# Layer 1's queries: projected already turned, for two tiles at once, in half steps, in three of its four groups

## The reference

```python
x = x + tanh(g_xattn[0]) * xattn0(layernorm(x), ctx, ...)     # 32 heads of 128, 8 kv heads, q and k normalized
x = x + tanh(g_ffn[0])   * lora(layernorm(x), ...)            # 8 experts of rank 16
x = x + tanh(g_xattn[1]) * xattn1(layernorm(x), ctx, ...)     # 16 heads of 96, 4 kv heads
x = x + tanh(g_ffn[1])   * ffn(layernorm(x), ...)             # silu(x Wg) * (x Wu), 1792 wide, then Wd
# xattn1: hidden = concat(context, latents)                   # 128 + 128 rows per batch
q = (latents @ Wq.T).reshape(b, q_len, H, HD)                 # H = 16, HD = 96
k = (hidden @ Wk.T).reshape(b, s_len, KV, HD)                 # KV = 4
v = (hidden @ Wv.T).reshape(b, s_len, KV, HD)
attn = softmax(einsum('bkgqd,bksd->bkgqs', q, k) / sqrt(HD))
out = einsum('bkgqs,bksd->bkgqd', attn, v) @ Wo.T
```

## Time and profile before

| | us |
|---|---|
| median of 3 runs | 1289.67 |
| lowest, highest | 1287.07, 1289.84 |
| the profiled execution | 1286.68 |
| its span, first to last instruction | 1284.9 |
| PE busy | 1254.5 (98%) |
| DVE busy | 962.4 (75%) |
| ACT busy | 830.0 (65%) |
| POOL busy | 583.7 (45%) |

### The profile page before, as it was taken

One profiled execution on the slowest core, in us unless ns is written; L12 is line 12 of the kernel. 1 busy time (PEld: TensorE's weight loads), 2 busy tenths in 40 slices (PEclk: granted clock), 3 DMA queues, 4 the chain that ended last, 5 costly groups with the idle time before them and its releaser, 6 DMA issues.

```text
span 1284.9 us, 24439 instructions
## 1 busy us (share of the span) xinstructions
PE 1254.5 (98%) x7392; PEld 1101.7 (86%) x7392; DVE 962.4 (75%) x2425; ACT 830.0 (65%) x2867; POOL 583.7 (45%) x1029
## 2 busy tenths in 40 slices
PE   8899999999999999999999989999999999999998
PEld 7788888888888888888888878889999999878886
DVE  7887777787777777777777888887777778963433
ACT  5777777777777777677777654566676666732221
POOL 4566556565565566555566542422333323540000
PEclk9899999999999999999999999999999999999999
DMA  6675566454554554654555332243543324370000
GB/s 181 127 128 119 90 128 117 99 119 103 124 105 103 118 115 87 134 112 84 122 114 116 83 70 42 67 77 60 103 92 74 78 60 104 72 176 1 33 1 33
DMA packets 339078, 121.11 MB, mean 94 GB/s; under 512 B 307104, under 2 KB 325280, under 8 KB 338976
## 3 DMA queue, kind: packets, MB, share of 16 engines
q1 hardware_dynamic: 313888, 84.59, 34.6%
q10 hardware_dynamic: 21104, 29.12, 7.9%
q0 software_dynamic: 3984, 6.29, 2.1%
HBM read 39.21 MB, written 2.10 MB: 32 GB/s over the span
## 4 chain that ended last, share of the span: by engine, by line
PE 52%; DVE 18%; ACT 13%; POOL 6%; DMA 6%; issue 5%; ACTq 0%; SPq 0%; DVEq 0%; POOLq 0%
PE bank L576 13%; PE bank L578 13%; PE bank L577 13%; PE bank L817 7%; DVE split L1220 6%; DMA turned<-scratch 4%; PE bank L835 4%; DVE scratch L1294 3%; ACT scratch L942 3%; POOL rq L1676 3%; ACT scratch L917 3%; ACT bank L905 3%; DVE mx L1303 3%; ACT pieces L954 2%; ACT split L871 1%
## 5 line engine op out<-in xcount | busy, mean ns | idle before, releaser
L576 PE MATMUL bank<-split 128*128 128x256 f32 (+6 forms) x2120 | 703.9, 332 | 14.5 <-DVE split L1220 8.4
L577 PE MATMUL bank<-split 128*128 128x256 f32 (+6 forms) x2120 | 692.4, 327 | 0.0
L578 PE MATMUL bank<-split 128*128 128x256 f32 (+6 forms) x2120 | 692.1, 326 | 0.0
L576 PEld LDWEIGHTS bank<-split 128*128 128x128 f32 (+2 forms) x2120 | 402.2, 190 | 63.7 <-DVE split L1220 18.6
L578 PEld LDWEIGHTS bank<-split 128*128 128x128 f32 (+2 forms) x2120 | 402.0, 190 | 35.1
L577 PEld LDWEIGHTS bank<-split 128*128 128x128 f32 (+2 forms) x2120 | 402.5, 190 | 31.0
L1657 POOL CAST split<-turned 128x512 fp32r<-128x512 f16 x384 | 234.3, 641 | 289.6 <-DMA turned<-pieces 287.8
L871 ACT ACTIVATE split<-bank 96x256 fp32r<-96x256 f32 (+6 forms) x392 | 165.1, 432 | 80.9 <-PE bank L671 44.8
L1220 DVE TENSOR_TENSOR split<-bank,split 96x256 fp32r<-96x256 f32 (+6 forms) x392 | 185.0, 474 | 26.1 <-ACT split L871 19.4
L942 ACT ACTIVATE scratch<-bank,nb,w_max 128x256 f32<-128x256 f32 x256 | 141.5, 564 | 73.3 <-DVE nb L1306 73.2
L1326 DVE SCALAR_TENSOR_TENSOR pieces<-scratch,rs,pieces 128x256 f16<-128x256 f32 x384 | 175.0, 509 | 4.5 <-ACT pieces L954 2.2
(11 more groups left out here) (82 smaller groups left out, 1205.7 us busy)
## 6 DMA issues: line engine op xcount, KB each, us to landing
raw<-in_wq_a ACTq DMA_DIRECT2D x14, 512.0 KB, 4.3
raw<-in_wo_a ACTq DMA_DIRECT2D x14, 512.0 KB, 3.8
raw<-in_wkv_a ACTq DMA_DIRECT2D x7, 512.0 KB, 6.7
turned<-pieces SPq DMA_TRANSPOSE x192, 3.3
raw<-in_wq_c ACTq DMA_DIRECT2D x8, 384.0 KB, 3.3
craw<-in_ctx_t SPq DMA_DIRECT2D x8, 256.0 KB, 4.1
raw<-in_wo_c ACTq DMA_DIRECT2D x4, 512.0 KB, 3.5
split<-in_down_t POOLq DMA_DIRECT2D x2, 1024.0 KB, 5.5
```

What stands on the lines that cost most here:

```text
L576: pe.matmul(out, whi, mhi, start=start, stop=False)
L577: pe.matmul(out, whi, mlo, start=False, stop=False)
L578: return pe.matmul(out, wlo, mhi, start=False, stop=stop)
```

## The change

For tiles 0 to 7 of layer 1 (group 0) nothing changes in how q is made. For the 24 others, PE makes q already turned: the weights are stationary and two tiles of x, 256 columns, move. There are 3 chunks of 128 output rows: heads 0 to 2, each with 32 rows of head 3 under it. That is 36 matmuls for two tiles, 18 in the step whose b+3 is even (`q_turned(..., 0)`) and 18 in the next (`q_turned(..., 1)`), into banks 6 and 3. `q_evac`, `q_turn`, `qt_evac` and `qt_low` are not called for them. In the second step of a pair ACT copies both tiles' q by five instructions (`qt_two_evac`: 96 rows x 512, 96 x 256, three of 32 x 256), DVE subtracts by five (`qt_two_low`), and the scores of the next step use the first of the two tiles.

So that the stationary chunks lie side by side, each weight block is written in two parts, 3x96 and 3x32 columns, by ACT, DVE and POOL alike. In layer 1 the blocks of a new group come in the order 3, 0, 1, 2 on ACT, all ahead of `o_evac`; DVE makes 0 and 1 before the residual add and 2 after it; POOL makes 3 before the cast of the next probabilities.

In the last group `norm_turn` stands behind `values`, `norm_hi` behind `o_evac`, `norm_low` behind `o_low`. In the step (3, 5), where no q is left to project, `k_turn` also stands behind `values`, `k_evac` behind `probs_high` and `k_low` behind `probs_low`.

```diff
+def by_rows(L, g, b):
+    return L is L1 and isinstance(g, int) and g * NT + b < NT
...
+        qT_two = split[:, qT_at:spot[0]].rearrange("p (s w h q) -> p w h s q", s=2, w=2, q=P)
...
+        def qT_moves(L):
+            rest = P - L.hd
+            first, last = chunks(bank[6][:, :], 2), bank[3][:, 0:2 * P]
+            heads = [(slice(0, L.hd), slice(0, 2), first[0:L.hd].rearrange("p c (s q) -> p c s q", s=2)),
+                     (slice(0, L.hd), slice(2, 3), last[0:L.hd].rearrange("p (c s q) -> p c s q", c=1, s=2))]
+            for c, src in enumerate((first[L.hd:P, 0, :], first[L.hd:P, 1, :], last[L.hd:P, :])):
+                heads.append((slice(rest * c, rest * (c + 1)), slice(L.oc, NH),
+                              src.rearrange("p (c s q) -> p c s q", c=1, s=2)))
+            return heads
...
+            def q_turned(L, g, b, half):
+                s = attn[L.name]
+                gb, tile = g + b // NT, b % NT
+                if half == 0:
+                    pe.wait_ge(s.qlo_done, q_low_written(*earlier(L, g, b)[1:]))
+                for c in range(L.oc):
+                    out = bank[6][:, c * 2 * P:(c + 1) * 2 * P] if c < 2 else bank[3][:, 0:2 * P]
+                    for k in range(KC):
+                        if (c * KC + k >= L.oc * KC // 2) != bool(half):
+                            continue
+                        if tile == 0 and c == 0 and k == 3:
+                            pe.wait_ge(s.wq_lo, q_blocks(L, gb, 1, 1))
+                        if tile == 0 and c == 0 and k < 3:
+                            pe.wait_ge(s.wq_lo_rest, q_blocks(L, gb, 3, k + 1))
+                        at_c = k * L.qw + c * P
+                        last = mm3(out, tuple(flat(w)[:, at_c:at_c + P] for w in wq),
+                                   at(xT, slice(None), k, slice(tile * P, (tile + 2) * P)),
+                                   start=k == 0, stop=k == KC - 1)
+                if half:
+                    last.then_inc(s.q_done, 1)
...
-                if three is not None:
+                if three is not None and (three[0] is L0 or by_rows(*three)):
                     q_proj(*three)
-                if two is not None and two[0] is L1:
+                elif three is not None and three[2] % 2:
+                    q_turned(*two, 1)
+                elif three is not None:
+                    q_turned(*three, 0)
+                if two is not None and two[0] is L1 and three is not None:
                     k_turn(*two)
-                if beside_norm is not None and beside_norm[0] > 1:
-                    norm_turn(*beside_norm)
...
                 values(L, g, b, second)
+                if two is not None and two[0] is L1 and three is None:
+                    k_turn(*two)
+                if beside_norm is not None and beside_norm[0] > 1:
+                    norm_turn(*beside_norm)
...
+            def qt_two_evac(L, g, b):
+                s = attn[L.name]
+                act.wait_ge(s.q_done, q_projected(g, b))
+                for rows, heads, src in qT_moves(L):
+                    copy(qT_two[rows, 0, heads], src).then_inc(s.qthi_done, 1)
...
+            def qt_two_low(L, g, b):
+                s = attn[L.name]
+                dve.wait_ge(s.qthi_done, q_low_written(g, b))
+                for rows, heads, src in qT_moves(L):
+                    low(qT_two[rows, 1, heads], src, qT_two[rows, 0, heads]).then_inc(s.qlo_done, 1)
...
             def q_lo(L, g, k):
                 s = attn[L.name]
-                sl = slice(k * L.qw, (k + 1) * L.qw)
-                dve.wait_ge(s.wq_hi, g * KC + (k + 1))
-                low(flat(wq[1])[:, sl], raw_q[:, sl], flat(wq[0])[:, sl]
-                    ).then_inc(s.wq_lo_rest, 1)
+                dve.wait_ge(s.wq_hi, q_blocks(L, g, KC, q_block_place(L, g, k)))
+                for out, in_, hi in zip(q_block(L, g, wq[1], k), raw_q_block(L, g, k), q_block(L, g, wq[0], k)):
+                    low(out, in_, hi).then_inc(s.wq_lo_rest, 1)
```

More of the change, by code:

```diff
@@ L775, in step @@
                     project(*prev, beside_norm)
-                if three is not None and three[0] is L1:
+                if three is not None and by_rows(*three):
                     q_turn(*three)
@@ L974, in q_hi @@
                 act.wait_ge(s.in_q, g * 32 + 32)
-                sl = slice(k * L.qw, (k + 1) * L.qw)
-                copy(flat(wq[0])[:, sl], raw_q[:, sl]).then_inc(s.wq_hi, 1)
+                for out, in_ in zip(q_block(L, g, wq[0], k), raw_q_block(L, g, k)):
+                    copy(out, in_).then_inc(s.wq_hi, 1)
             def o_hi(L, g, c):
@@ L1074, in step @@
                         probs_high(*one, 1)
-                if beside_norm is not None and beside_norm[0] > 1:
-                    norm_hi(*beside_norm)
+                    if three is None and two is not None:
+                        k_evac(*two)
                 if L is L0 and b == 0:
@@ L1448, in step @@
                     probs_low(*one, 1)
+                if three is None and kv is not None:
+                    k_low(*kv)
                 if new_o and not is_at(L, g, L0, 0):
@@ L1454, in step @@
                     k_low(*kv)
-                if beside_norm is not None and beside_norm[0] > 1:
-                    norm_low(*beside_norm)
+                if three is not None and three[0] is L1 and not by_rows(*three) and three[2] % 2:
+                    qt_two_low(*two)
                 if lora is not None:
@@ L1471, in step @@
                     norm_scale(*next_norm)
-                if new_q is not None and not ahead:
+                if new_q is not None and L is L0 and not ahead:
                     q_lo(*new_q, 0)
@@ L1477, in step @@
                     q_lo(*new_q, 0)
-                if three is not None and three[0] is L1:
+                if three is not None and by_rows(*three):
                     qt_low(*three)
-                if new_q is not None:
+                if new_q is not None and L is L0:
                     q_lo(*new_q, 1)
@@ L1483, in step @@
                     o_low(L, g, b)
-                if new_q is not None:
+                if beside_norm is not None and beside_norm[0] > 1:
+                    norm_low(*beside_norm)
+                if new_q is not None and L is L0:
                     q_lo(*new_q, 2)
@@ L1750, in step @@
                     norm_rstd(3, NT - 4)
+                if new_q is not None and L is L1:
+                    q_lo(*new_q, 3)
                 if one is not None:
@@ L1809, in _ @@
             cast_probs(L1, g, NT - 1, 1)
[L1810 removed]
+            pool.wait_ge(attn[L1.name].q_done, q_projected(L1.groups - 1, NT - 1))
             pool.dma_start(down_mid, down_src[:, MD:ME, :]).then_inc(in_ff[2], 16)
```

78 lines of the change are left out of this document (57 added, 21 removed).

## The result

The changed kernel takes 1297.22 us in the median of 11 runs (1294.23 to 1303.74), the kernel before beside it 1289.2 (1285.55 to 1292.2): ratio 1.0071, 95% interval 1.0053 to 1.0088, which is 9.2 us of 1289.2. The profiled executions differ by 9.7 us (1296.38 against 1286.68).

What follows compares the result with a forecast made beforehand. PE was taken as the bound, busy for all of a 10.29 us step, with DVE's room shrinking towards the end. Terms: -8.4 + 1.4 + 4.8 + 1.1 = -1.1, + 6.4 - 0.7 = +4.6; 1294.3 us, forecast 1292 to 1298, range 1284 to 1300.

Steps and rivals of the forecast that it cites:

- Relief on PE: PE's steps for 24 tiles: q transposes go, projection becomes 18 matmuls; 0.35 us saved a tile, 8.4 us in all.
- rival D: PE's q projection: 18 weight loads outlast their matmuls, so no relief and the end's 5.7 stays; 1295.4 us, chance 0.01.
- Five subtractions and copies: Second step of a pair: DVE's five subtractions take 2.40 us (bounds 2.04 and 2.50), ACT's five copies 2.09.
- Rival A: No change: subtractions overlap (2.04) or ACT is 0.3 us quicker, so ordinary scores don't wait; 1289.6 us, chance 0.22.
- Ordinary pairs: Six pairs of steps each end with PE waiting 0.23 us for the scores: +1.4 us.
- Weight steps: Steps (1,4) and (2,4), which also make new q blocks, make DVE late and PE wait: 2.4 us each, +4.8.
- Last group: Normalization adds 2.0 us to DVE's step; (3,2) ends late and (3,3) waits 0.3 + 0.8: +1.1 us.
- Up to (3,5): Sum of the relief and the groups' waits up to the start of step (3,5): -1.1 us.
- The end: First gate matmul late by DVE's lateness 3.9 and the moved subtraction 3.5, less 1.0 idle: +6.4 us.
- Later waits: PE's waits after the first gate matmul, 0.42 and 0.3 us, become hidden by its lateness: -0.7 us.
- Rival B: Faster: DVE's lateness in (3,4) and (3,5) never reaches the gate matmul; 1285.7 or 1283.1 us, chance 0.19.
- Rival C: Worse: five copies or subtractions take a tenth more, weight steps pass lateness on; about +10, 1300 us, chance 0.10.

Runs made afterwards that it cites:

- e1_each: Changed kernel, with DVE waiting before each of its five q subtractions only for the copies sharing its bank and rows; ratio to the kernel before 1.0016.
- e3_tail_alone: Kernel before, with only the last group's moves added and no turned q; ratio to the kernel before 1.0015.
- e2_tail_old: Changed kernel, with the last group's moved work (normalized tiles, and k in (3,5)) put back in its old place; ratio to the kernel before 1.0050.
- c3_tail_norm: c1_each_first_tail, but k's move in (3,5) kept as in the changed kernel; ratio to the kernel before 0.9974.
- c2_each_first: Changed kernel with e1_each's waits and q blocks 0 and 1 ahead of the turned q's copies and subtractions; 1286.59 us, ratio to the kernel before 0.9983.
- e4_pool_later: Changed kernel, with POOL's casts of the probabilities waiting for DVE's blocks 0 and 1 where new q blocks are made; ratio to the kernel before 1.0076.
- c1_each_first_tail: c2_each_first with the last group's moved work back in its old place; 1283.74 us, ratio to the kernel before 0.9964.
- c4_tail_k: c1_each_first_tail, but the normalized tiles' moves kept as in the changed kernel, only k's undone; ratio to the kernel before 0.9981.

## Why the prediction was right, and where not

Forecast +4.6 us, slower by 2.7 to 8, gate matmul 17 us behind (3,5). Measured: +9.2 by the ratio, above that range, and +8.0 by the medians, at its edge; 1297.22 us itself lies in the 1292 to 1298 stated. The sign and the gate matmul's place (17.39) were right, and so was the mechanism, DVE's lateness; a term in the groups was too small by 3.5 us.

- **Relief on PE**: forecast 0.35 us a tile. With DVE in time a pair takes 9.94 + 9.92 = 19.86 us (e1_each), before 20.58: 0.36 a tile. Right, and rival D with it is out.
- **Five subtractions and copies**: forecast 2.40 and 2.09, measured 2.39 and 2.06. Rival A rested on the subtractions overlapping. In the trace after, only the second does, by 0.08 us; the three of 32x256 each start 0.03 behind the end of the one before. So three of the five hold back, not the four that the prediction counted; the sum comes out the same.
- **Ordinary pairs**: forecast 6 x 0.23 = 1.4. Against before less 0.36, seven steps are 0.14 to 0.38 long, 2.1 together. That the wait for all five copies makes them, e1_each shows, but for (1,1).
- **Weight steps**: this is the step that failed. Forecast 2.4 each (1.5 of it in the step itself), measured 14.12 - 9.96 = 4.16 each, 8.3 and not 4.8. I took a block on DVE at 0.66, with 0.86 as the upper bound, from the earlier trace rows (mean 0.706). Blocks 0 and 1 took 1.6 each. The mean hid two kinds: in layer 1's groups of the trace of before a block takes 0.55 us with POOL still and 0.70 to 1.43 beside it. The change puts the blocks, earlier in DVE's queue, beside POOL's own block, its four casts and the k and v block, and I counted only DVE's instructions. The page "SBUF — State Buffer" of the Trainium skill, section Who interferes with whom, has it: a DVE instruction with two inputs in SBUF contends with a GpSimd instruction that reads SBUF. By that rule the blocks are held and the subtractions from a bank are not; the trace agrees with both (96x384 from a bank: 0.55 us beside POOL and without). The forecast's list of waits also lacked the one at the k and v projection, 0.79.
- **Last group**: forecast 1.1, measured 1.0 in (3,3) and 0.1 in (3,4). Another 0.7 in (3,1) isn't DVE's: PE waits there for nothing that the profile shows, and it stays in e1_each (10.74 us for the step), where DVE is in time.
- Up to (3,5): forecast -1.1, measured +3.3.
- **The end**: forecast +6.4, measured +6.58. The size is right, its parts are less so. I had 3.9 for DVE's lateness, 3.5 for the moved subtraction, less 1.0 of idle time. The moves alone are 3.9 us (e3_tail_alone), the rest without them 4.7 (e2_tail_old); together 6.6 and not 8.6. Part of the 4.7 is the clock (above), so the two can't simply be added, and the 3.9 of DVE's lateness alone was not measured. Undoing the moves wins 1.9 to 2.3 at the gate matmul, where the forecast had them at 2.5.
- **Later waits**: forecast -0.7, measured 5.75 - 6.58 = -0.83, and that is luck. The waits that were to be hidden (0.42 and 0.30) are gone, as forecast. But the 16 gate matmuls took 5.36 us where c3_tail_norm takes 3.65, 1.7 lost to the clock (below). From the gate matmul to the end of PE's last it is 165.55 us after and 165.23 before, 0.3 more. The rest of the -0.83 lies behind PE's last matmul: 4.6 us to the end of the span, 5.8 before. The last store, issued at the same distance, lands sooner there. This holds for all nine kernels with the turned q, and e3_tail_alone has the 5.8 of the kernel before; why, no run shows.

Rival B (faster) made its case depend on the five subtractions of (3,4) ending by 2.6 us of (3,5). In the changed kernel they end at 3.34. In c2_each_first they end at 1.57, and (0,4) to (3,5) takes 253.8 us, 6.2 less than before. But the end still costs 4.9 (186.75 us), where B had 1.8. So the gain of the groups is real once the blocks' cost is taken away, and B's price for the end was too low. Rival D stood among the chances of no change, though its own time was 5.7 us slower; at 0.01 that changes nothing. Rival C stood at +10, which is nearer to the ratio's 9.2 than my 4.6; but its mechanism, copies or subtractions a tenth longer, didn't happen, and the lateness that the weight steps passed on came from POOL.

## What to carry to other kernels

Before a table's mean becomes a term, split it by what the other engines did: here one instruction took 0.45 or 0.85 us by whether POOL ran beside it. When work moves within one queue, look at what stands beside its new place, not only at what stands behind it. And a wait for the last of several producers deserves a look by itself: taking it apart, two lines of code, was worth about 7 us, and with two blocks in the gap so found a slower kernel became one faster than both.

## What the runs showed of the hardware

DVE's subtractions with both sources in SBUF (`raw`, `split`) take longer beside POOL. In the trace after, 128x288 took 0.45 us with POOL idle and 0.81 in the mean beside it, 128x96 0.25 and up to 1.04. ACT beside them changes nothing (0.45 in e4_pool_later). Not every block beside POOL is slow: at 860.47 in e3_tail_alone a 128x384 took 0.56, and POOL's own block of that size, which started with it, took 1.42 in place of 1.0. It works the other way too: POOL's casts, mostly 0.61 us, take up to 0.83 beside a block.

A late wait at the end can cost twice, which I had not forecast. The changed kernel's stretches of 2 us behind its waits of 2.16 and of 2.02 us:

```profile
1115.00:1117.00 2.00, 2.00 (x8) 1.31 (x7) 1.75 (x3) 0.81 (x3) 2.00 (x4) 0.50 0.00 0
...
1125.00:1127.00 2.00, 2.00 (x6) 1.61 (x5) 0.99 (x2) 0.00 (x0) 2.00 (x5) 0.50 0.00 0
```

The granted clock is 0.50 there, 1.2 GHz, and matmuls of 512 columns start 0.427 us apart in place of 0.227. In both cases PE had idled 0.50 to 0.63 us shortly before, and then 2.0 to 2.2. In c1_each_first_tail, waits of 1.23 and 0.39 us (rows above) were enough; behind the single wait of 3.73 us in c4_tail_k the 16 gate matmuls took 5.36 too. The waits of 1.08 and 0.70 in (1,5) left the clock at 1.00, and so did a single one of 2.06 in c3_tail_norm:

```profile
1106.00:1108.00 2.00, 1.67 (x10) 1.33 (x11) 1.51 (x4) 1.09 (x5) 2.00 (x5) 1.00 0.00 0
```

What tells these cases apart, the runs don't show.
